# Graph attention on one core: row sums inverted on GpSimd, blocks finished in pairs, W scaled ahead of all products

## What is computed

```
h  = relu(layernorm(x))                         # x: 8 x 2048 x 256
Wh = h @ W;   f1 = Wh @ a1;   f2 = Wh @ a2      # W: 256 x 256
e  = leaky(f1[:, :, None] + f2[:, None, :])     # slope 0.2 below zero
attention = softmax(where(adj > 0, e, -9e15), axis=1)
x + elu(attention @ Wh)                         # adj: 8 x 2048 x 2048
```

## Time and profile before

| | |
|---|---|
| median of 3 runs | 1094.68 us (1094.28 to 1096.93) |
| profiled execution | 1092.74 us, span 1091.0 us |
| busy PE, DVE, ACT | 972.8, 978.4, 958.3 us |
| busy POOL | 401.7 us |
| granted TensorE clock, mean | 0.984 of 2.4 GHz |
| DMA queue of the loads and stores | 62.2% of 16 engines' span |

### The profile page before, as it was taken

How to read it: one execution, slowest core, us unless ns; L and a number is a source line. 1 busy time by engine, 2 the same in 40 slices (tenths; PEclk the granted TensorE clock), 3 DMA queues, 4 the chain that set the end, 5 groups by cost and what they waited for, 6 DMA issues and landing times. The chain is left out here.

```text
span 1091.0 us, 24411 instructions
## 1 busy us (share of the span) xinstructions
PE 972.8 (89%) x8963; PEld 831.9 (76%) x8963; DVE 978.4 (90%) x1579; ACT 958.3 (88%) x1606; POOL 401.7 (37%) x317
## 2 busy tenths in 40 slices
PE   4667799899999999899998999999999999888987
PEld 3445688788878888787887888787887878777776
DVE  4379999999999999999999999999999999999973
ACT  3368999999999999998999999998999989988974
POOL 2313323334343433334343343334333343333334
PEclk9769999999999999999999999999999999999999
DMA  4366665666676676666766666766766566766614
GB/s 129 113 184 168 167 174 163 193 181 193 190 207 181 180 217 180 189 179 197 200 190 197 180 195 188 208 176 186 211 191 186 172 192 171 198 179 184 180 35 150
DMA packets 325654, 195.11 MB, mean 179 GB/s; under 512 B 9760, under 2 KB 321312, under 8 KB 325536
## 3 DMA queue, kind: packets, MB, share of 16 engines
q1 hardware_dynamic: 325536, 193.56, 62.2%
HBM read 176.69 MB, written 16.84 MB: 177 GB/s over the span
## 5 line engine op out<-in xcount | busy, mean ns | idle before, releaser
L689 POOL TENSOR_TENSOR direct<-prob,inv 128x1024 f16<-128x1024 f32 x128 | 242.6, 1895 | 590.7 <-DVE inv L605 585.2
L589 DVE CUSTOM_DVE_ANT_0 prob<-tp,f_row 128x2048 f32<-128x2048 bf16 x128 | 293.3, 2291 | 4.9 <-issue 4.4
L378 PE MATMUL acc<-v,direct 128*128 128x256 f16 x1024 | 280.2, 274 | 11.1 <-DVE direct L613 6.0
L360 PE MATMUL acc_st<-v,stored 128*128 128x256 f16 x992 | 270.2, 272 | 22.2 <-DVE z_st L629 21.6
L380 PE MATMUL acc<-v,direct 128*128 128x256 f16 x1024 | 279.9, 273 | 0.0
L382 PE MATMUL acc<-v,direct 128*128 128x256 f16 x1024 | 279.9, 273 | 0.0
L362 PE MATMUL acc_st<-v,stored 128*128 128x256 f16 x992 | 270.3, 272 | 0.0
L361 PE MATMUL acc_st<-v,stored 128*128 128x256 f16 x992 | 270.3, 272 | 0.0
L439 ACT ACTIVATE prob<-prob,shift 128x2048 f32<-128x2048 f32 x128 | 256.6, 2005 | 10.8 <-issue 0.4
L432 ACT ACTIVATE prob<-prob,f 128x2048 f32<-128x2048 f32 x128 | 255.6, 1997 | 0.0
L331 PEld LDWEIGHTS tp<-ident_b,neg 128*128 128x128 bf16 x2048 | 119.5, 98 | 94.1 <-issue 92.1
(11 more groups left out here) (71 smaller groups left out, 1222.4 us busy)
## 6 DMA issues: line engine op xcount, KB each, us to landing
raw<-in_adj SPq DMA_DIRECT2D x128, 1024.0 KB, 6.0
x_in<-in_x SPq DMA_DIRECT2D x128, 128.0 KB, 5.0
y<-in_x SPq DMA_DIRECT2D x128, 128.0 KB, 4.6
out<-y SPq DMA_DIRECT2D x128, 128.0 KB, 3.7
f_row<-f_scratch SPq DMA_DIRECT2D x32, 256.0 KB, 5.0
f_scratch<-f_t SPq DMA_DIRECT2D x128, 0.5 KB
w_cat<-in_W SPq DMA_DIRECT2D x1, 256.0 KB, 2.9
prob<-in_a SPq DMA_DIRECT2D x1, 256.0 KB, 3.7
```

The lines of the kernel that those rows point to most:

```text
L360: nc.tensor.matmul(bank[:, 0:FO], p_st[:, 0, rows], v_c[:, 0, :], start=(c == 0), stop=False)
L378: nc.tensor.matmul(acc[:, m, :], p_d[:, 0, rows], v_c[:, 0, :], start=(j == 0 and m % 2 == 0), stop=False, skip_group_check=True)
L589: nc.vector.tensor_tensor_reduce(out=prob[:, c % 2, :], in0=tp_b, in1=f1_row[:, b % 2, :], scale=1.0, scalar=-3.0e38, op0=ALU.add, op1=ALU ...
L689: nc.gpsimd.tensor_tensor(direct[:, c % 2, 0, :], p[:, 0:HALF], k.to_broadcast([P, HALF]), ALU.mult).then_inc(hi_direct, 1)
```

## The change

The change has five parts.

1. **The inverse sum moves from DVE to POOL.** `reciprocal` and `scale_inverse` are gone from DVE. POOL's `split_high(c)` now begins with two instructions of 128x1: total times 2^-14, and that to the power -1.
2. **Blocks are finished in pairs.** `finish_relu`, `finish_exp`, `finish_elu`, `finish_add` and the two DMAs of a block work on two blocks at once (128x512), half as often; `ORDER` places a pair in steps 2, 3, 5, 7, 9, 11, 13 and 15 of a batch.
3. **W is scaled once.** One DVE instruction multiplies W by `tops[5]` before the first `Wh`; after that ACT's `split_v_high` is a plain copy and DVE's `split_v_low` a plain subtraction.
4. **DVE's order.** After `mask_scores(s)` come `add_halves`, `statistics`, `aggregate`, `split_v_low`, in place of `statistics`, `split_v_low`, `add_halves`, `aggregate`.
5. **Buffers.** RX 7 to 6 (and x is loaded one step later), RZ 3 to 4, RY 8 single to 4 double, RE 4 single to 2 double, `h_t` from two buffers to one in the main part.

The diff, cut to its core:

```diff
-    RX = 7
+    RX = 6
-    RY = 8
-    RZ = 3
-    RE = 4
+    RY = 4
+    RZ = 4
+    RE = 2
...
+        def h_buf(c):
+            return h_t_early if c < LEAD and c % 2 else h_t[:]
...
-        ORDER = {2: [0, 8], 3: [1], 4: [2], 5: [3, 9], 6: [4], 7: [5], 8: [6], 9: [7],
-                 10: [10], 11: [11], 12: [12], 13: [13], 14: [14], 15: [15]}
-        ORDER_LAST = {2 + q: [q, 8 + q] for q in range(8)}
+        ORDER = {2: [4], 3: [0], 5: [1], 7: [2], 9: [3], 11: [5], 13: [6], 15: [7]}
+        ORDER_LAST = {2: [4], 3: [0], 4: [5], 5: [1], 6: [6], 7: [2], 8: [7], 9: [3]}
...
-                if chunk(s + 25) and s + 25 >= RX:
-                    load_x(s + 25)
+                if chunk(s + 24) and s + 24 >= RX:
+                    load_x(s + 24)
...
                 if c == 0:
                     pe.wait_ge(w_ready, 4)
+                    pe.wait_ge(w_scaled, 1)
...
-                nc.scalar.activation(v[:, c % RV, 0, :], wh_bank(c)[:, 0:FO], ACT.Copy, scale=k_in).then_inc(v_hi, 1)
+                nc.scalar.copy(v[:, c % RV, 0, :], wh_bank(c)[:, 0:FO]).then_inc(v_hi, 1)
...
-                wait(act, recip_s, c - R + 1)
+                wait(act, total_s, c - R + 1)
...
-                nc.vector.tensor_scalar(tops[:, 5:6], tops[:, 3:4], W_TOP, None, ALU.mult).then_inc(k_ready, 1)
+                link(nc.vector.tensor_scalar(tops[:, 5:6], tops[:, 3:4], W_TOP, None, ALU.mult))
+                nc.vector.tensor_scalar(w_nat, w_nat, tops[:, 5:6], None, ALU.mult).then_inc(w_scaled, 1)
...
-                nc.vector.scalar_tensor_tensor(out=v[:, c % RV, 1, :], in0=wh_bank(c)[:, 0:FO], scalar=k_in,
-                                               in1=v[:, c % RV, 0, :], op0=ALU.mult, op1=ALU.subtract
-                                               ).then_inc(v_ready, 1)
-
-            def reciprocal(c):
-                dve.wait_ge(prob_ready, c + 1)
-                nc.vector.reciprocal(inv_total[:, c % R:c % R + 1], total[:, c % R:c % R + 1]).then_inc(recip_s, 1)
-
-            def scale_inverse(c):
-                dve.wait_ge(recip_s, c + 1)
-                nc.vector.tensor_scalar(inv[:, c % R:c % R + 1], inv_total[:, c % R:c % R + 1], 2.0 ** P_BITS, None,
-                                        ALU.mult).then_inc(inv_ready, 1)
+                nc.vector.tensor_tensor(v[:, c % RV, 1, :], wh_bank(c)[:, 0:FO], v[:, c % RV, 0, :], ALU.subtract
+                                        ).then_inc(v_ready, 1)
...
             for s in range(FIRST, END + 2):
                 if chunk(s):
                     mask_scores(s)
-                if chunk(s + 23):
-                    statistics(s + 23)
-                if chunk(s + LEAD):
-                    split_v_low(s + LEAD)
                 n = block_at(s - 1)
                 if n is not None and not first_half(n):
                     add_halves(n)
                 if chunk(s + 23):
+                    statistics(s + 23)
                     aggregate(s + 23)
+                if chunk(s + LEAD):
+                    split_v_low(s + LEAD)
...
-                if chunk(s):
-                    reciprocal(s)
-                    scale_inverse(s)
...
             def split_high(c):
                 p = prob[:, c % 2, :]
                 k = inv[:, c % R:c % R + 1]
+                t = small_total[:, c % R:c % R + 1]
+                pool.wait_ge(prob_ready, c + 1)
+                nc.gpsimd.tensor_scalar(t, total[:, c % R:c % R + 1], 2.0 ** -P_BITS, None, ALU.mult).then_inc(total_s, 1)
+                pool.wait_ge(total_s, c + 1)
+                wait(pool, lo_stored, c - R + 1)
+                nc.gpsimd.tensor_tensor(k, t, minus_one[:], ALU.pow).then_inc(inv_ready, 1)
                 pool.wait_ge(inv_ready, c + 1)
...
-                nc.gpsimd.tensor_tensor(y[:, k % RY, :], y[:, k % RY, :], elu[:, k % RE, :], ALU.add
-                                        ).then_inc(y_ready, 1)
+                pair = y[:, k % RY].rearrange("p t f -> p (t f)")
+                nc.gpsimd.tensor_tensor(pair, pair, elu[:, k % RE, :], ALU.add).then_inc(y_ready, 1)
```

More of the change, by code:

```diff
@@ L69, in graph_attention @@
         z_st = sb("z_st", [P, RZ, FO], F32)
-        elu = sb("elu", [P, RE, FO], F32)
+        elu = sb("elu", [P, RE, 2 * FO], F32)
         x_in = sb("x_in", [P, RX, F], F32)
-        y = sb("y", [P, RY, FO], F32)
+        y = sb("y", [P, RY, 2, FO], F32)
         xn = sb("xn", [P, 2, F], F32)
-        h_t = sb("h_t", [P, 2, KC, P], F32)
+        h_t = sb("h_t", [P, KC, P], F32)
         f12 = sb("f12", [P, 64 + RF], F32)
@@ L83, in graph_attention @@
         ones = prob[0:1, 0, 1024:1024 + P]
+        h_t_early = prob[:, 1, 1024:1024 + F].rearrange("p (k c) -> p k c", k=KC)
         w_nat = w_cat[:, :, 0:FO]
@@ L92, in graph_attention @@
         minus_half = sb("minus_half", [P, 4], F32)
+        minus_one = sb("minus_one", [P, 1], F32)
         top = sb("top", [P, R], F32)
@@ L96, in graph_attention @@
         total = sb("total", [P, R], F32)
-        inv_total = sb("inv_total", [P, R], F32)
+        small_total = sb("small_total", [P, R], F32)
         inv = sb("inv", [P, R], F32)
@@ L123, in graph_attention @@
         w_max_all = sem("w_max_all")
-        k_ready = sem("k_ready")
+        w_scaled = sem("w_scaled")
         w_times_a = sem("w_times_a")
@@ L134, in graph_attention @@
         prob_ready = sem("prob_ready")
-        recip_s = sem("recip_s")
+        total_s = sem("total_s")
         inv_ready = sem("inv_ready")
@@ L161, in graph_attention @@
         f_ready = sem("f_ready")
-        k_in = tops[:, 5:6]
         k_out = tops[:, 4:5]
@@ L226, in finish, with rows_of @@
             return finish_at.get(s, [])
-        def output_rows(k):
+        def rows_of(tensor, k):
             b, i = finishing[k]
-            r = (NB + i if i < NB else i - NB) * P
-            return b, slice(r, r + P)
+            r = (NB + 2 * i if i < 4 else 2 * (i - 4)) * P
+            return tensor[b, r:r + 2 * P, :].rearrange("(t p) f -> p t f", p=P)
         def h_prime(k):
             b, i = finishing[k]
-            return z_st[:, i % RZ, :] if i < NB else z_direct[:, i - NB, :]
+            z = z_st[:, 2 * i % RZ:2 * i % RZ + 2, :] if i < 4 else z_direct[:, 2 * (i - 4):2 * (i - 4) + 2, :]
+            return z.rearrange("p t o -> p (t o)")
         finish_index = {item: k for k, item in enumerate(finishing)}
@@ L287, in _ @@
                     wait(sp, y_out[k % RY], 16 * (k // RY))
-                    bo, rows = output_rows(k)
-                    sp.dma_start(y[:, k % RY, :], x[bo, rows, :]).then_inc(x_res_in[k % RY], 16)
+                    sp.dma_start(y[:, k % RY], rows_of(x, k)).then_inc(x_res_in[k % RY], 16)
                 for k in finish(s - 2):
                     sp.wait_ge(y_ready, k + 1)
-                    bo, rows = output_rows(k)
-                    sp.dma_start(out[bo, rows, :], y[:, k % RY, :]).then_inc(y_out[k % RY], 16)
+                    sp.dma_start(rows_of(out, k), y[:, k % RY]).then_inc(y_out[k % RY], 16)
                 if chunk(s + LEAD) and (s + LEAD) % 4 == 3:
@@ L296, in _ @@
             for i in range(RY):
-                sp.wait_ge(y_out[i], 16 * (B * C // RY))
+                sp.wait_ge(y_out[i], 16 * (len(finishing) // RY))
         @block.tensor
@@ L307, in make_wh @@
                 for k in range(KC):
-                    last = nc.tensor.matmul(wh_bank(c)[:, 0:FW], h_t[:, c % 2, k, :], w_cat[:, k, :],
+                    last = nc.tensor.matmul(wh_bank(c)[:, 0:FW], h_buf(c)[:, k, :], w_cat[:, k, :],
                                             start=(k == 0), stop=(k == KC - 1))
@@ L449, in make_h @@
                 act.wait_ge(xt_ready, c + 1)
-                wait(act, wh_ps, c - 1)
-                nc.scalar.activation(h_t[:, c % 2].rearrange("p k c -> p (k c)"), xt_bank(c)[:, 0:F], ACT.Relu
+                wait(act, wh_ps, c - 1 if c < LEAD else c)
+                nc.scalar.activation(h_buf(c).rearrange("p k c -> p (k c)"), xt_bank(c)[:, 0:F], ACT.Relu
                                      ).then_inc(ht_ready, 1)
@@ L466, in take_direct @@
                 act.wait_ge(direct_done, C * (b + 1))
-                wait(act, elu_ready, C * b)
+                wait(act, elu_ready, G * b)
                 m = slice(4 * h, 4 * h + 4)
@@ L475, in finish_relu @@
                 wait(act, y_ready, k - RE + 1)
-                if i < NB:
-                    act.wait_ge(z_stored, G * b + i + 1)
+                if i < 4:
+                    act.wait_ge(z_stored, G * b + 2 * i + 2)
                 else:
@@ L626, in add_halves @@
                 if past >= 0:
-                    k_past = finish_index[(past // G, past % G)]
+                    k_past = finish_index[(past // G, past % G // 2)]
                     dve.wait_ge(elu_ready, k_past + 1)
@@ L674, in _ @@
             nc.gpsimd.memset(minus_half[:], -0.5)
+            nc.gpsimd.memset(minus_one[:], -1.0)
             nc.gpsimd.memset(ones, 1.0)
```

3 lines of the change are left out of this document (removed).

## The result

| | before | after |
|---|---|---|
| median | 1094.48 us (4 runs, 1091.88 to 1096.93) | 1057.70 us (4 runs, 1055.98 to 1060.47) |
| profiled execution | 1092.74 us, span 1091.0 | 1057.97 us, span 1056.2 |
| busy PE, DVE, ACT, POOL | 972.8, 978.4, 958.3, 401.7 us | 961.3, 958.8, 938.5, 513.1 us |

The ratio is 0.9667, with a 95% interval of 0.9636 to 0.9697. The forecast was 1061 us; the kernel is 36.8 us faster by the medians, for 32 in the sum.

The account below looks back on a forecast made before the run. No engine alone bounds it: PE, ACT and DVE form a ring, DVE having the most work. Middle -28, first batch -2, last steps -5, head +2.5, tail +0.5 sum to -32 from 1092.7: 1061 us stated, range 1044 to 1086.

Parts of the forecast that it names:

- The middle: Chunks 17 to 111, 5.9 batches of 16 chunks: a batch falls from 127.1 to 122.3 us, 28 us off.
- the ring: PE makes Wh, ACT splits it, DVE behind it is held up, PE waits for DVE; 1.2 us a batch left.
- PE has the same work: PE's own work in a batch stays 119.3 us; its 3.7 us wait for z_st should nearly go.
- The collision: POOL's longer pair addition runs into DVE's split: 0.35 us for each of 8 pairs, 2.8 us a batch on.
- The inverse: On POOL, latency 1.15 us with a power of 0.6; ACT stalls 2.0 us a batch waiting for it.
- The slower rival: ACT stands at the inverse at L445 in every step, with a power of 2.0 us: 1150 us, chance 0.12.
- Half the gain: Inverse 0.4 us late, from a 1.0 us power or POOL waiting for the mask's end: 1079 us, chance 0.20.
- PE alone is the bound: Rival with a power of 0.35 us and no collisions, a batch of 119.3 and 0.5: 1041 us, chance 0.08.
- No change: Two stalls together eat the gain, for instance latency 1.6 with 0.52 lost every pair; 3 us or less left, chance 0.03.
- The signs: Batch 121 to 124 us, v wait under 1.5, z_st wait nearly gone, L445 waits 0.3 to 0.6 in bare steps.
- First batch and last 16 steps: First batch: steps of 7.05 us, 2 us off in all; last 16: steps of 6.9 for 7.22, 5 off.
- The head and the sum: Head 2.5 us on: 1.2 for scaling W, 1.3 for one x buffer less; all terms sum to -32 us.

Follow-up runs that it names:

- short_add: Changed kernel with POOL's addition of a pair taking in only 32 of 512 columns, x missing from the rest: 1049.6 us, ratio 0.9583.
- power_only: Changed kernel without POOL's 2^-14 product before the power, so the attention part comes out smaller by 2^14: 1048.2 us, ratio 0.9584.
- new_order_only: Kernel before with only DVE's new order (add_halves, statistics, aggregate, split_v_low): 1078.9 us, ratio 0.9845.
- pool_inverse_only: Kernel before with only the inverse moved to POOL, blocks single and DVE's old order: 1087.0 us, ratio 0.9931.
- two_powers: Changed kernel with POOL's power made twice, one after the other with a semaphore between, so the inverse comes later: 1101.9 us, ratio 1.0069.

## Why the prediction held, and where it didn't

- **The middle** was forecast at 122.3 us a batch and took 122.1. Own work, the batch less the engine's waits: PE 117.7 (119.3 forecast), DVE 119.0 (121.1), ACT 118.9 (119.9). Each is 1 to 2 us lower than said, and the ring keeps more of it: the waits for v were put at 1.2 us and are 3.0. Two errors of opposite sign, which cancel; that the batch came out within 0.2 us is luck. The "1.2 us left in the ring" is the step that had no row behind it. "PE has the same work" was wrong by 1.6 us: with the same matmuls PE's busy time in one batch is 119.1 us before, 117.7 after and 117.1 with the short addition, so it isn't a fixed amount of work, and why it differs is open.
- **DVE's terms.** The collision, 0.35 for a pair, measured 0.39 against the shortened addition. The longest splits are longer than the 1.5 to 1.8 us expected (2.02, and up to 2.28 in the run), but other pairs hardly meet the split. "The plain subtraction I cost at nothing" was wrong: 410 ns for 482, a gain of 1.2 us a batch. The statistics and the aggregate right behind them cost less than the 1.6 us forecast: from start to start, without waits, the two take 9.5 us a batch for 8.6 before, 0.9 on. And DVE's own work before was put too high by a wait that the earlier trace rows leave out:

```profile
DVE inv_total L601 <- ACT prob L439: 0.3, 1, 0.3
```

With these, 121.1 - 1.2 - 0.7 - 0.3 + 0.3 for the collision gives 119.2, for 119.0 measured.
- **The inverse.** Power 0.57 for 0.6 forecast; product 0.22 alone for 0.15, but 0.37 on the mean, since it often starts inside a DVE instruction and waits for its end. In the first batch ACT stands 0.23 us a step at L445, in the middle 1.4 us a batch, for 2.0 forecast: three steps wait 0.57, 0.32 and 0.51 us, for 0.49 each in the sum, and no other step waits, for 0.13 in four. This term was sized from rows and came within 0.6 us.
- **The slower rival** named L445 as the place and a latency of 1.7 us, a power of 1.15, as the point from which it decides. Two powers of 0.57 and 0.55 with a handoff are 1.20 us (516.23 - 515.03), and that kernel is 0.7% slower than before. The mechanism is shown, and the point is borne out as far as two kernels can: 0.57 us on one side, 1.20 on the other, and nothing was run between.
- **Half the gain** had as its second condition that POOL's small instructions wait for the end of the mask. They do (L678 above, and L677 at 0.50 us and more in the change), but for some tenths of a us in some steps, not in all.
- **The other rivals.** "PE alone is the bound" asked for a power of 0.35 and no collisions; the power takes 0.57 and a collision 0.39. Nor did taking the collision away make PE the bound: in short_add a batch of 121.2 us holds 117.1 of PE's work and 4.1 of its waits. "No change" needed a latency of 1.6 us with 0.52 lost at every pair; the latency is 1.0 us in the first batch, and the longest wait of the middle, 0.57 us, makes it about 1.2.
- **The signs.** A batch, PE's wait for z_st and the waits at L445 came as named. DVE's wait for v did not: under 1.5 us was named, 3.0 came.
- **First batch and last 16 steps** were off by 4.6 and 3.1 us, in opposite directions. In the first batch a step takes 6.81 us (111.27 - 104.46) for 7.05, and the chain of the inverse shows why:

```profile
104.59 0.18 ACT L439 ACTIVATION_READ_ACCUMULATOR prob<-prob,shift 128x1 f32 x1
...
104.86 0.22 POOL L677 TENSOR_SCALAR small_total<-total 128x1 f32<-128x1 f32 x1 [3.97 <-ACT prob L439]
...
105.16 0.57 POOL L680 TENSOR_TENSOR inv<-small_total,minus_one 128x1 f32<-128x1 f32 x1
...
105.76 1.15 ACT L445 ACTIVATE stored<-prob,inv 128x1024 f16<-128x1024 f32 x1 [0.23 <-POOL inv L680]
```

The latency is 105.76 - 104.77 = 0.99 us instead of 1.15: POOL stands behind nothing here, so the 0.2 us for DVE's elu doesn't apply. ACT's wait still sets the step, for with the product left out (power_only) it is 6.6 to 6.7 us. Ten steps of the first batch take 68.3 us for 72.5, of which 1.5 is the first step, and the next seven take 2.4 less; the forecast had 1.2 and 1. In the last steps the forecast took 6.9 us; they alternate between 6.95 and 7.35, and with the short addition they take 3.5 us less. The collision was counted for the middle and only touched on here.
- **The head and the sum.** The first product with W starts at 12.92 us for 11.28, 1.6 on for 1.2 forecast, and chunk 0 starts 1.5 later for 2.5. Since chunk 0 starts at 61.9 to 64.6 us in the three kernels whose head is that of before (before, new_order_only, pool_inverse_only), this one difference tests nothing. The sum gave 1060.7 against the profiled execution and added that the median is 1.9 higher, which would be 1062.6; the 1061 stated leaves it off.
- **Parts without a number of their own.** The sum had the new order only as "PE's 3.7 should nearly go" and "1.2 left in the ring". It is the dearest part to lose, 23.5 us. That parts 1 and 4 are worth so much more together than apart stands nowhere in the forecast. The pairs were costed at a gain of 1.8 us a batch for ACT and DVE against 2.8 of collision, and so they turned out, no gain or a loss of 5 us.

The Trainium skill (GPSIMD Engine Reference, Specifications) was weighed for its contention with DVE instructions in a 2-port mode. That the mask runs in such a mode isn't in the trace, but POOL's product does wait for the mask's end (0.76 us for 0.22). The same skill (SBUF — State Buffer, SBUF: two separate sides) says that whichever engine starts first keeps the shared ports for its whole instruction and the other fully blocks. The rows agree in both directions: in two_powers the product ends 0.08 us after the mask, and in the change the split ends 1.09 us, nearly its full 1.28, after the addition.

## What to carry to other kernels

Where several engines run a ring in which each is at work for 94 to 98% of a step, time taken off one of them is worth little until the order in which it meets its waits is right: the freed 5.4 us a batch gave 7 us of the run alone and 21 us with the new order and the other parts in place. Before moving small work to a slower engine, read two latencies there: how late it comes for the engine that waits, and what it pushes behind itself, here an addition pushed into another engine's two-input instruction. Combining small instructions saves their starts but makes longer obstacles; measure the single form beside it.

## What the runs showed of the hardware

- POOL's power on 128x1 takes 0.57 us and on 128x4 1.01 with no DVE instruction in its way, so some 0.15 a column on 0.42 (an estimate from these two). POOL's product on 128x1 takes 0.22 us alone and up to 0.87 in the change.
- Where a POOL and a DVE instruction collide, the later one bears it. When POOL comes first, POOL's addition takes 1.26 to 1.29 us in all 64 cases of the change and DVE's split up to 2.28 for 1.28. When DVE comes first, POOL's power on 128x4 takes 1.98 for 1.01. POOL's multiplication (1.89 us) holds up a DVE addition of 128x512 too, 1.12 us for 0.72, but it runs beside DVE's score instruction with neither longer (1.89 and 2.28).
- A delay of 0.65 us on a 1 us path cost 44 us in 128 steps, 0.34 a step, although the path was hardly waited for (1.4 us a batch).
- Not settled: why the start of chunk 0 varies from 61.9 to 68.1 us between profiled executions of nearly the same head; what holds a batch at 121.1 us; and whether single blocks beat pairs by 5 us or by nothing.
